# Cross-attention stage of a four-block kernel: one mask transfer per slot, key parts a step later in two buffers, the transposed maxima copied by ScalarE

## The reference, cut to what matters

```
x = x + self_attention(adaln(x))        # rotary positions on q, k; 16 heads of 8
x = x + cross_attention(adaln(x), ctx)  # q from x; k, v from the 1500 context rows
x = x + mlp(adaln(x))                   # 128 -> 512 -> 128, gelu
```

## Time and profile before

| | us |
|---|---|
| median of 3 runs | 6056.02 (6052.6 to 6056.93) |
| the profiled execution | 6043.84 |
| its span, first to last instruction | 6042.0 |
| TensorE busy in the span | 5595.8 (93%) |
| VectorE, ScalarE, GpSimd busy | 3779.0, 3230.0, 2247.7 |
| granted TensorE clock, mean | 0.965 of full speed |

### The profile page before, as it was taken

The page is one execution under the profiler, slowest core; times in us unless marked ns, Lnnn a source line. Parts: engine busy times, 40 slices in busy tenths (PEclk is TensorE's granted clock), DMA queues, the critical chain, the costliest instruction groups (busy, mean ns, idle before and its releaser), DMA issues.

```text
span 6042.0 us, 140669 instructions
## 1 busy us (share of the span) xinstructions
PE 5595.8 (93%) x55893; PEld 4177.1 (69%) x55893; DVE 3779.0 (63%) x8627; ACT 3230.0 (53%) x6405; POOL 2247.7 (37%) x2204
## 2 busy tenths in 40 slices
PE   5899999999999999999799999998799999989997
PEld 4667667677676676776457778776477777756984
DVE  3888888887887888888553444444544444444553
ACT  1566666666766766667543344443333333324764
POOL 4666666666666666656200000000011111156440
PEclk7999999999999999999898999999799999998998
DMA  2776776776767767768400100001000000030000
GB/s 63 120 118 106 119 120 104 120 116 107 125 110 115 121 109 116 121 107 130 92 11 10 42 32 32 30 29 33 11 11 16 11 16 11 11 105 24 1 1 25
DMA packets 396485, 407.85 MB, mean 68 GB/s; under 512 B 125575, under 2 KB 372946, under 8 KB 393786
## 3 DMA queue, kind: packets, MB, share of 16 engines
q1 hardware_dynamic: 395834, 398.85, 37.6%
HBM read 158.00 MB, written 0.46 MB: 26 GB/s over the span
## 4 chain that ended last, share of the span: by engine, by line
PE 62%; POOL 8%; SPq 7%; DVE 7%; issue 7%; ACT 5%; DMA 3%; POOLq 1%; DVEq 0%; ACTq 0%
PE psum L2276 11%; PE psum L2243 10%; PE psum L1575 5%; PE psum L1587 4%; PE psum L2288 4%; PE psum L1561 4%; SPq L1475 4%; POOL slot_context L3476 3%; PE psum L1723 2%; PE psum L1609 2%; PE psum L1601 2%; SPq L1493 2%; PE psum L416 2%; PE psum L430 2%; DVE row_max L1940 2%
## 5 line engine op out<-in xcount | busy, mean ns | idle before, releaser
L1940 DVE TENSOR_REDUCE row_max<-psum 112x1 f32<-112x500 f32 x2304 | 1443.3, 670 | 185.2 <-PE psum L1575 170.4
L2067 ACT ACTIVATE weights<-psum 125x448 f32<-125x448 f32 x2304 | 1140.8, 541 | 521.2 <-PE psum L1561 514.6
L1575 PE MATMUL psum<-key_stack,query_stack 97*128 97x500 bf16 x2304 | 874.6, 380 | 111.0 <-DMA query_stack<-query_parts 51.1
L1561 PEld LDWEIGHTS psum<-query_stack,key_stack 121*128 121x128 bf16 x9216 | 654.1, 99 | 370.9 <-issue 184.6
L1561 PE MATMUL psum<-query_stack,key_stack 121*128 121x112 bf16 x9216 | 837.6, 213 | 33.2 <-ACT weights L2067 27.9
L2356 DVE TENSOR_REDUCE l_stat<-psum 128x1 f32<-128x1500 f32 (+1 forms) x224 | 391.7, 1749 | 544.9 <-PE psum L2243 544.9
L2276 PE MATMUL psum<-l_ctx_v,l_turned 125*128 125x128 f32 x5376 | 713.7, 281 | 16.4 <-ACT l_turned L2314 12.2
L2276 PEld LDWEIGHTS psum<-l_ctx_v,l_turned 125*128 125x128 f32 x5376 | 643.1, 191 | 59.2 <-ACT l_turned L2314 40.2
L1587 PE MATMUL psum<-weights,values 125*17 125x112 f32 x18432 | 553.9, 261 | 0.0
L1587 PEld LDWEIGHTS psum<-weights,values 125*17 125x17 f32 x18432 | 408.0, 97 | 144.1 <-issue 141.2
L2314 ACT ACTIVATE l_turned<-psum 125x512 f32<-125x512 f32 x448 | 251.3, 597 | 434.9 <-PE psum L2288 432.1
(11 more groups left out here) (539 smaller groups left out, 10182.9 us busy)
## 6 DMA issues: line engine op xcount, KB each, us to landing
key_stack<-key_parts SPq DMA_DIRECT2D x1728, 125.0 KB, 4.6
ctx_t<-in_ctxT SPq DMA_DIRECT2D x96, 750.0 KB
l_ctx_v<-in_ctxV SPq DMA_DIRECT2D x32, 750.0 KB
query_stack<-query_parts SPq DMA_DIRECT2D x576, 28.0 KB, 3.5
l_ctx_t<-in_ctxT SPq DMA_DIRECT2D x16, 750.0 KB
slot_context<-in_ctxV SPq DMA_DIRECT2D x16, 750.0 KB
key_stack<-ctx_mask_rows SPq DMA_DIRECT2D x576, 3.9 KB
sm_w<-in_sm_w SPq DMA_DIRECT2D x3, 2048.0 KB
```

Source lines behind the costliest of these rows:

```text
L1561: mm = e.matmul(self.k.psum[:, h, (p % 4) * QC:(p % 4 + 1) * QC], ks[:, at:at + 128], q[:, p * QC:(p + 1) * QC])
L1575: e.matmul(self.k.psum[:, 2 + n % 2, 0:500], q[0:ROWS_MAX, p * QC:p * QC + 128], ks[0:ROWS_MAX, p, c * 500:(c + 1) * 500]).then_inc(self.m ...
L1940: e.tensor_reduce(self.largest[:, i % PAIRS, i // PAIRS:i // PAIRS + 1], k.psum[0:QC, 2 + i % 2, 0:500], AX.X, ALU.max, negate=True).then_ ...
L2067: e.activation(half(self.p[kt % RING_P], h), self.k.psum[0:KN, h, 0:HALF], ACT.Exp).then_inc(self.exped.sem, 1)
```

## The change

- The mask rows are kept as 16 rows of 1500 in place of 96 rows of 250, and one DMA per slot takes the place of six.
- SyncE issues the queries ahead of keys piece 1 in place of ahead of keys piece 2.
- `key_temp` becomes two buffers. VectorE fills one when lo of the piece before the last is done. Hi moves from two to three steps after the key, rest with it, mid and lo from three to four. Where GpSimd has steps of two pieces, the older goes first.
- The copy of the transposed maxima goes to ScalarE, ahead of the exponentials of step 11.
- `divide` becomes two instructions. The transposes ahead of it write two of their four outputs eight columns further left, so that one access pattern reaches all heads.

```diff
-            for n in range(6):
-                e.dma_start(dst[ROWS:ROWS + 1, :, n * 250:(n + 1) * 250],
-                            self.mask_rows[6 * b + n:6 * b + n + 1, :].unsqueeze(1).broadcast_to(
-                                [1, PAIRS, 250])).then_inc(self.mask_stacked.sem, 16)
+            e.dma_start(dst[ROWS:ROWS + 1, :, :],
+                        self.mask_rows[b:b + 1, :].unsqueeze(1).broadcast_to([1, PAIRS, L])).then_inc(
+                            self.mask_stacked.sem, 16)
...
             if 0 <= s + 2 < NS:
+                self.stack_queries(e, s + 2)
                 self.stack_keys(e, s + 2, 1)
...
             if 0 <= s + 2 < NS:
-                self.stack_queries(e, s + 2)
                 self.stack_keys(e, s + 2, 2)
...
-                tr = e.transpose(side.bank(*key)[0:S, i * 128:(i + 1) * 128], self.acc[:, i * S:(i + 1) * S],
-                                 k.ident[:, :])
+                at = i * 128 - 8 * (i % 2)
+                tr = e.transpose(side.bank(*key)[0:S, at:at + 128], self.acc[:, i * S:(i + 1) * S], k.ident[:, :])
...
+        sums = bk.rearrange("p (g c) -> p g c", g=2)[:, :, 0:240].rearrange("p g (h c) -> p g h c", h=2)
+        e.reciprocal(inv.rearrange("p (g h j) -> p g h j", g=2, h=2), sums[:, :, :, 0:97:32]).then_inc(inverted.sem, 1)
         e.wait_ge(inverted.sem, value)
+        e.tensor_tensor(o.rearrange("p (m d) -> p m d", d=8), bk.rearrange("p (m c) -> p m c", c=32)[:, :, 1:9],
+                        spread(inv, 8), ALU.mult).then_inc(side.emptied(*key), 1)
...
-            if (b, c) > (0, 0):
-                e.wait_ge(self.key_lo.sem, self.key_lo(b, c) - 1)
+            if (b, c) > (0, 1):
+                e.wait_ge(self.key_lo.sem, self.key_lo(b, c) - 2)
+            bk, tm = side.bank(*key)[:, 0:500], self.tm[(3 * b + c) % 2]
...
-    def rows_vector(self, e, b):
+    def rows_scalar(self, e, b):
...
+        e.activation(self.q_stack[b % 3][ROWS:ROWS_ALL, :].rearrange("r (p c) -> r p c", p=PAIRS),
+                     rows.unsqueeze(1).broadcast_to([1 + 3 * PAIRS, PAIRS, QC]), ACT.Copy).then_inc(
+                         self.side.emptied(*key), 1)
...
-        hi = {2: (s + 2, 1), 6: (s + 2, 2), 10: (s + 3, 0)}.get(kt)
-        mid = {3: (s + 2, 1), 7: (s + 2, 2), 11: (s + 3, 0)}.get(kt)
+        hi = {3: (s + 2, 1), 7: (s + 2, 2), 11: (s + 3, 0)}.get(kt)
+        mid = {4: (s + 2, 1), 8: (s + 2, 2), 0: (s + 2, 0)}.get(kt)
...
             for kt in range(KT):
+                if 0 <= s + 1 < NS and kt == 11:
+                    self.rows_scalar(e, s + 1)
                 for h in range(2 if 0 <= s < NS else 0):
...
-        for late in range(1, 4):
+        for late in (4, 3, 1):
...
-            if late == 2:
+            if late == 3:
                 e.wait_ge(self.key_hi.sem, self.key_hi(b, c))
...
-            if late == 3:
+            if late == 4:
                 e.wait_ge(self.key_mid.sem, self.key_mid(b, c))
```

More of the change, by code:

```diff
@@ L1279, in __init__ @@
             self.bias = sb("l0_bias", [128, NL, 5])
-            self.mask_rows = sb("ctx_mask_rows", [6 * B, L // 6], BF16)[:, :]
+            self.mask_rows = sb("ctx_mask_rows", [B, L], BF16)[:, :]
             self.src_mask = sb("src_mask", [TALL, T], BF16)[:, :]
@@ L1290, in __init__ @@
             self.q_tmp = sb("query_block", [128, 2, QC])
-            self.tm = sb("key_temp", [128, 2, 500])
+            self.tm = [sb(f"key_temp{i}", [128, 2, 500]) for i in range(2)]
             self.ctx_t = [sb(f"ctx_t{i}", [128, L])[:, :] for i in range(2)]
@@ L1313, in __init__ @@
                 self.src_mask8 = k.sb(s2, "src_mask8", [1, T], U8)[:, :]
-                self.ctx_mask8 = k.sb(s2, "ctx_mask8", [6 * B, L // 6], U8)[:, :]
+                self.ctx_mask8 = k.sb(s2, "ctx_mask8", [B, L], U8)[:, :]
         self.tables_arrived = ev("l0_tables_arrived", step=112)
@@ L1328, in __init__ @@
         self.part_stacked = [ev(f"key_part{i}_stacked", NS * 3 // 2, step=16 * len(K_PARTS)) for i in range(2)]
-        self.mask_stacked = ev("key_mask_stacked", NS, step=96)
+        self.mask_stacked = ev("key_mask_stacked", NS, step=16)
         self.q_stacked = [ev(f"query_stack{i}_arrived", NS // 3, step=16 * len(Q_PARTS)) for i in range(3)]
@@ L1509, in sync @@
         e.dma_start(self.parity, dr["head_parity"]).then_inc(sem, 16)
-        e.dma_start(self.ctx_mask8, dr["ctx_mask"]).then_inc(sem, 16)
+        e.dma_start(self.ctx_mask8, dr["ctx_mask"].rearrange("(b n) c -> b (n c)", b=B)).then_inc(sem, 16)
         e.dma_start(self.bias[:, :, :], dr["l0_bias"]).then_inc(sem, 16)
@@ L1739, in phase_tensor @@
                 for m in range(4):
-                    tr = e.transpose(side.bank(*key)[0:S, m * 128:(m + 1) * 128], self.sacc[:, m * S:(m + 1) * S],
-                                     k.ident[:, :])
+                    at = m * 128 - 8 * (m % 2)
+                    tr = e.transpose(side.bank(*key)[0:S, at:at + 128], self.sacc[:, m * S:(m + 1) * S], k.ident[:, :])
                 tr.then_inc(side.filled, 1)
@@ L1817, in fixed_vector @@
             e.wait_ge(side.filled, side.at(*key))
-            if (b, c) > (0, 0):
-                e.wait_ge(self.key_lo.sem, self.key_lo(b, c) - 1)
-            bk = side.bank(*key)[:, 0:500]
-            e.stream_shuffle(self.tm[:, 1, :], bk, OTHER_HALF).then_inc(self.key_turned.sem, 1)
-            e.tensor_tensor(self.tm[:, 0, :], bk, self.cos[:, cols], ALU.mult).then_inc(side.emptied(*key), 1)
+            if (b, c) > (0, 1):
+                e.wait_ge(self.key_lo.sem, self.key_lo(b, c) - 2)
+            bk, tm = side.bank(*key)[:, 0:500], self.tm[(3 * b + c) % 2]
+            e.stream_shuffle(tm[:, 1, :], bk, OTHER_HALF).then_inc(self.key_turned.sem, 1)
+            e.tensor_tensor(tm[:, 0, :], bk, self.cos[:, cols], ALU.mult).then_inc(side.emptied(*key), 1)
         if 1 <= s <= NS and kt == 2:
@@ L1933, in vector @@
                     self.max_parts_vector(e, s + 1)
-                if 0 <= s + 1 < NS and kt == 11:
-                    self.rows_vector(e, s + 1)
                 if self.max_at(s, kt):
@@ L1965, in fixed_scalar @@
                 e.wait_ge(self.part_stacked[n % 2].sem, self.part_stacked[n % 2](n // 2 - 1))
-            e.activation(self.k_part[n % 2][:, 0, :], self.tm[:, 0, :], ACT.Copy).then_inc(self.key_hi.sem, 1)
+            e.activation(self.k_part[n % 2][:, 0, :], self.tm[n % 2][:, 0, :], ACT.Copy).then_inc(self.key_hi.sem, 1)
         if mid and 0 <= mid[0] < NS:
@@ L1969, in fixed_scalar @@
             e.wait_ge(self.key_rest.sem, self.key_rest(b, c))
-            e.activation(self.k_part[(3 * b + c) % 2][:, 1, :], self.tm[:, 1, :], ACT.Copy).then_inc(self.key_mid.sem, 1)
+            e.activation(self.k_part[(3 * b + c) % 2][:, 1, :], self.tm[(3 * b + c) % 2][:, 1, :], ACT.Copy).then_inc(self.key_mid.sem, 1)
         if 0 <= s + 2 < NS and kt == 2:
@@ L2074, in key_gpsimd @@
     def key_gpsimd(self, e, s, kt):
-        tm, side = self.tm, self.side
-        for late in range(1, 4):
+        side = self.side
+        for late in (4, 3, 1):
             if kt < late:
@@ L2083, in key_gpsimd @@
             b, c = at
-            part = self.k_part[(3 * b + c) % 2]
+            part, tm = self.k_part[(3 * b + c) % 2], self.tm[(3 * b + c) % 2]
             if late == 1:
```

12 lines of the change are left out of this document (removed).

## The result

The change made the kernel slower: median 6099.26 us (6095.17 to 6108.06, four runs) against 6054.31 us (6052.0 to 6056.93, four runs) of the kernel before, ratio 1.0076, 95% interval 1.0059 to 1.0094. That is 45 us more, where I forecast 31 less; it lies outside the range. The profiled execution took 6108.06 us, 64 more than that of before.

The account below looks back on a forecast made before the run. In Block0, TensorE was taken as nearly full in heavy slots, SyncE and DMA queues as pacing light ones. Terms -41 - 26 + 45 + 5 - 16 + 0 + 2 = -31 us gave 6025 us, range 5955 to 6080.

Parts of the forecast that it names:

- part 1: Light slots: one mask transfer and queries ahead of key piece 1 make queries land sooner; -41 us (0 to -51).
- Part 2, heavy places: Self-attention slots (places 2 to 4 of eight): GpSimd's lo delays the rotation, then l_qd; +45 us (0 to +97).
- rival D: Heavy places: all eight l_qd of a period lack slack, +97 in place of +45, 6077 us; chance 0.17.
- Rival B: Heavy places lose nothing, slack absorbing the shift, and light places' waits all go: -93 us, 5963 us; chance 0.21.
- Part 2, light places: Places 1 and 5: hi waits 2.3 us less for GpSimd, TensorE feels about half; -26 us (0 to -51).
- P: Experiments' name: ScalarE's hi copy waits for key piece 1 to land, because the queries are issued ahead of it.
- S: Experiments' name: with later key steps, lo stands directly before the next rotation on GpSimd, so l_qd is late.
- Part 3: Maxima copy moved to ScalarE: +5 us there (0 to +86), -16 us from relieving VectorE (0 to -44).
- rival F: Light slots: the maxima copy on ScalarE counts around step 11, +25 in place of +5, 6045 us; chance 0.04.
- Rival E: One 24 KB mask transfer lands later than six small ones and TensorE waits for it: 6056 us; chance 0.02.
- Part 4: Divide in two instructions on VectorE: 0 us, hidden under TensorE's matmuls; up to -20 if VectorE limits next.
- Rival C: DMA engines bound the light places: part 1 brings only -15, sum -5, 6051 us, no change; chance 0.14.

Follow-up runs that it names:

- L_qd first: Changed kernel with GpSimd making l_qd (elements 1 to 7) ahead of the key's rotation, two key_parts buffers kept: 6036.94 us, ratio 0.9977.
- three buffers: Changed kernel with three key_parts buffers in place of two, mask bytes sharing a weights buffer: 6045.37 us, ratio 0.9987.
- both cures: Changed kernel with three key_parts buffers and l_qd (elements 1 to 7) ahead of the rotation on GpSimd: 5995.35 us, ratio 0.9901.
- three buffers, old steps, VectorE: Changed kernel with three key_parts buffers, key steps as before the change and the maxima copy back on VectorE: 5999.97 us, ratio 0.9912.

## Why the prediction was wrong, point by point

**The step that failed: part 1.** The prediction put down -41 us and one sentence behind it: the issues of piece 1 now come later, and L1966 in step 11 waits for their landing. It gave that sentence no price, though its last line named it as what would make the forecast wrong. The runs give the part in two: the mask alone -23 us, the queries ahead of piece 1 +73, together +50. The instants to price it were at hand in the trace of before: the hi copy that refills piece 1's buffer starts 10.9 us (median; 7.3 in the tightest tenth) after the last issue of piece 1 has ended, and the page gives 4.6 us from issue to landing. That leaves 6.3 and 2.7 us of slack. Six query issues and the wait for q_lo then pushed piece 1 back by 5.4 us (median, the kernel with mask and early queries), so in the tight slots hi waits. The landing holds a buffer, the buffer holds hi, and hi holds the exponentials behind it. I checked who waits for the queries and who reads the keys, not who waits for the keys' source to come free. All the other terms together were forecast at +10 us, and between the kernel with mask and early queries and the changed one the medians show -1. So part 1, 91 us off, makes the whole miss of 76 and more; the rest came out some 11 us better than forecast.

**Part 2, heavy places: right in kind, somewhat too small.** +45 us forecast, +59 found (1190.2 for 1131.5 us). L_qd first (62 us back, or 50 us when three buffers are there) does a little more than undo this: it brings places 2 to 4 to 1123.6 us, 8 below before. The rotation came 1.1 us late, as worked out. Forecast for L1718's wait: from 15.5 to about 60 us; it is 70.3. Nearly all of the 88 waited (77), so rival D's count was nearer than mine. Its price (+97) was too high: the wait rose by 54.8 us, 0.6 us for each of 88, since part of the 1.1 us met slack. Rival B, in which slack takes up all of it, is out.

**Part 2, light places: -26 forecast, the size came out by luck.** Outside places 2 to 4 the later steps, with the copy and the divide, give 42 us back, where these parts were forecast at -37. But the road is another. Hi's wait for the rotation did fall by 75 us, as forecast, yet where P and S are away this is worth nothing that can be measured (5995.35 us with the later steps, 5989.73 without): half of a wait on ScalarE was priced as TensorE's, with no row behind the half. What the later steps brought here was relief from P, the cost that part 1 had made: hi's wait for landings is 80.7 us with them, and 116.6 in the kernel with mask and early queries.

**Part 3: -11 forecast in sum, not resolved.** The copy took 905 ns in the changed kernel:

```profile
L1830 ACT ACTIVATE query_stack<-psum 25x896 bf16<-25x896 bf16 x96 | 86.9, 905 | 2.4
```

0.90 was worked out from smaller copies. The two pairs that differ in it alone (6099.26 and 6102.32; 5989.73 and 5999.97) both lean its way, by 3 and 10 us, inside their noise. Neither leans towards rival F, which wanted the copy to count; its price, +25 in place of +5, is too near the noise of one pair to be ruled out by it. (Rival E is out: the tables of waits of the changed kernel and of the one with the mask alone have no row for the mask.) The Trainium skill ("ScalarE: Activation LUTs", "Rules for kernel authors") names relu, max, min, add and mul as work for VectorE, the faster engine; read as a rule for a plain copy too, by the engine's time the trace agrees (905 against 618 ns), by the kernel's time neither pair does. Only where hi stalls in front of it did the place of the copy matter (187.3 us of waits in the kernel with the old key steps).

**Part 4: 0, and none found that can be told from noise** (6106.29 us with the old divide, 6099.26 with the new). The multiply is 282 ns where four of 175 stood, and TensorE waited for it once, 0.7 us.

**Once only:** the mask scaling takes 3985 ns where 5.2 us were worked out; nothing in the sum hangs on it.

**Rival C, the DMA engines as the bound, is out.** The mask alone gave 23 us with the same bytes, and with both cures places 7, 0 and 1 run at a DMA share of 0.90 and 79.0 us, where before they ran at 0.79 and 82.2, with SyncE off the chain. Five of the last slots, of the kind of the earlier trace rows, went from 117.6 to 112.6 us. So a share of 0.98 was not yet the bound. It may be the next one: place 0 alone shows a share of 1.00 in the kernel with both cures. No run tests that.

**Small slips.** The profiled execution took 6043.84 us, not 6043.82, and place 2 takes 37.9 us, not the 37.8 of its last paragraph; neither moves the sum.

**Open.** Waits explain less than the whole: the next section. That both orders of queries and piece 1 are bad was shown with two buffers and the later steps only. Queries late with three buffers was not tried, so no run shows whether the early queries are worth anything in the best kernels. The second `key_temp` was never taken away alone.

## What to carry to other kernels

When a transfer is moved ahead in a queue that runs in order, price three parties for the one pushed back: who reads what it writes, who refills what it reads, and what stands behind that refill on its engine. The wait that decides need not be on an engine that the diff touches. If two orders in one queue both make someone late, look for a buffer rather than an order: here a third one gave 54 us back.

## What I had not expected of the hardware

A stall seems to cost more than its length. TensorE's busy time in Block0, same matmuls, and the time from 200 us to the end of Block0 that the trace's clock record shows at the lower level (1.2 GHz, half of full speed). The records of matmuls differ by up to 68 of some 37,850, so busy times are good to a few us:

| kernel | busy us | idle us | at half clock us |
|---|---|---|---|
| three buffers, old steps, VectorE | 2655.5 | 97.5 | 0 |
| mask only | 2658.1 | 134.9 | 17 |
| before | 2657.6 | 148.4 | 20 |
| both cures | 2668.9 | 88.1 | 55 |
| changed | 2693.5 | 176.5 | 89 |
| queries behind piece 1 | 2710.6 | 243.4 | 178 |

Against before, the changed kernel has 28 us more idle time and 36 more busy time; 68 us more at half speed would make an estimated 34. So more than half of its loss in Block0 is not in any row of waits. One such stretch of the changed kernel, in steps of 4 us:

```profile
1256.00:1260.00 4.00, 4.00 (x79) 3.29 (x77) 3.53 (x7) 3.05 (x8) 3.52 (x4) 1.00 0.09 18
1260.00:1264.00 4.00, 2.80 (x28) 2.53 (x27) 1.04 (x3) 0.61 (x2) 2.07 (x2) 1.00 0.16 33
1264.00:1268.00 4.00, 4.00 (x53) 2.69 (x51) 2.39 (x5) 2.20 (x6) 1.13 (x1) 0.57 1.03 146
```

TensorE was busy 2.80 of 4 us, and in the next 4 us the granted clock is 0.57 while it has work all the time. No run changed the clock without changing the waits, so its own price is a reading of these two columns, not a measurement. Two rows warn against a simple rule. With both cures the kernel still shows 55 us at half clock with the least idle time; and with the queries behind piece 1 the same estimate would give 79 us of extra busy time against before, where 53 are found.
